# Scores of three attentions in row tiles of 32 or 64 rows, two heads interleaved into two PSUM banks

## The reference, cut to what matters

```python
# layer 0: self attention over 112 tokens, 16 heads of 32, causal; then cross
# attention to a context of 375 positions, 16 heads of 16, no mask
scores = einsum('bhqd,bhkd->bhqk', q * scale, k)        # 112 x 112, then 112 x 375
# layers 1 and 3: cross attention to the same context, 16 heads of 64, key mask
sim = einsum('bhid,bhjd->bhij', q, k)                   # 112 x 375
sim = where(media_mask[:, None, None, :], sim, finfo.min)
attn = softmax(sim, axis=-1)
out = einsum('bhij,bhjd->bhid', attn, v)
```

## Time and profile before

| | |
|---|---|
| median of 3 runs | 2167.96 us (2167.66 to 2169.86) |
| the profiled execution | 2164.93 us, of which its span 2163.1 us |
| PE busy | 1976.2 us, 91% |
| DVE busy | 1286.9 us, 59% |
| POOL busy | 1185.7 us, 55% |
| ACT busy | 917.9 us, 42% |
| mean granted TensorE clock | 0.97 |

### The profile page before, as it was taken

The page is one execution under the profiler, slowest core; times in us unless marked ns, Lnnn a source line. Parts: engine busy times, 40 slices in busy tenths (PEclk is TensorE's granted clock), DMA queues, the critical chain, the costliest instruction groups (busy, mean ns, idle before and its releaser), DMA issues.

```text
span 2163.1 us, 35765 instructions
## 1 busy us (share of the span) xinstructions
PE 1976.2 (91%) x12332; PEld 1725.7 (80%) x12332; DVE 1286.9 (59%) x3174; ACT 917.9 (42%) x2326; POOL 1185.7 (55%) x1357
## 2 busy tenths in 40 slices
PE   4998888988899999999999989998879999998998
PEld 3865576777689998989999978996548999987998
DVE  6777766777545254347888845422175888874422
ACT  2025515555421121137777723222134777771321
POOL 3553417557078899966444336870045545423785
PEclk9999889999899999999999999999999999999999
DMA  3110100001023333321000022332230000001232
GB/s 119 39 55 1 38 15 8 15 21 31 22 76 101 116 109 116 115 76 40 9 20 12 12 82 78 108 108 65 77 102 25 20 13 22 13 2 40 88 108 83
DMA packets 38193, 118.88 MB, mean 55 GB/s; under 512 B 6168, under 2 KB 10264, under 8 KB 38016
## 3 DMA queue, kind: packets, MB, share of 16 engines
q1 hardware_dynamic: 31408, 107.92, 16.0%
q10 hardware_dynamic: 6608, 8.68, 1.3%
HBM read 114.75 MB, written 1.84 MB: 54 GB/s over the span
## 4 chain that ended last, share of the span: by engine, by line
PE 57%; DVE 21%; issue 9%; ACT 7%; POOL 4%; DMA 1%; ACTq 0%; DVEq 0%; SPq 0%; POOLq 0%
PE psum L542 9%; PE psum L543 9%; PE psum L544 9%; PE psum L535 6%; PE psum L804 6%; DVE masked_t L1319 4%; PE psum L658 4%; PE psum L660 4%; PE psum L659 4%; DVE kk L1285 3%; ACT probs_t L988 3%; DVE probs_t L1330 3%; PE psum L761 2%; POOL wl L1631 2%; ACT probsT_t L1006 1%
## 5 line engine op out<-in xcount | busy, mean ns | idle before, releaser
L1631 POOL TENSOR_TENSOR wl<-raw,wh 128x256 fp32r<-128x256 f32 x656 | 517.8, 820 | 13.7
L1623 POOL TENSOR_SCALAR wh<-raw 128x1024 fp32r<-128x1024 f32 x164 | 185.4, 1130 | 329.3 <-PE psum L544 181.5
L542 PE MATMUL psum<-nh,wh 128*128 128x448 f32 x904 | 348.6, 386 | 14.5 <-DVEq L1384 7.8
L543 PE MATMUL psum<-nl,wh 128*128 128x448 f32 x904 | 337.7, 374 | 0.0
L544 PE MATMUL psum<-nh,wl 128*128 128x448 f32 x904 | 337.0, 373 | 0.0
L761 PE MATMUL psum<-cst,probs_t 112*125 112x112 f32 (+1 forms) x1304 | 237.9, 280 | 58.0 <-DVE probs_t L1330 57.6
L988 ACT ACTIVATE probs_t<-masked_t,nmin 112x375 f32<-112x375 f32 (+1 forms) x384 | 205.9, 536 | 181.3 <-DVE nmin L1319 178.4
L761 PEld LDWEIGHTS psum<-cst,probs_t 112*125 112x125 f32 (+1 forms) x1304 | 189.4, 183 | 109.8 <-DVE probs_t L1330 106.1
L1330 DVE TENSOR_SCALAR probs_t<-probs_t,rinv 112x376 f32<-112x376 f32 (+1 forms) x520 | 249.9, 481 | 18.5
L1456 DVE TENSOR_TENSOR hid_l<-scr,hid_h 128x448 fp32r<-128x448 f32 x108 | 93.5, 866 | 229.1 <-ACT hid_h L1063 228.5
L542 PEld LDWEIGHTS psum<-nh,wh 128*128 128x128 f32 x904 | 175.5, 194 | 36.6 <-issue 11.1
(11 more groups left out here) (187 smaller groups left out, 4418.5 us busy)
## 6 DMA issues: line engine op xcount, KB each, us to landing
raw<-in_walls SPq DMA_DIRECT2D x183, 512.0 KB, 3.4
raw<-in_ctxF SPq DMA_DIRECT2D x24, 375.0 KB, 3.0
ctxb<-in_ctxF ACTq DMA_DIRECT2D x8, 375.0 KB, 3.9
ctxt<-in_ctxK ACTq DMA_DIRECT2D x8, 375.0 KB
x<-in_xT ACTq DMA_DIRECT2D x2, 896.0 KB, 11.1
outT<-x SPq DMA_DIRECT2D x2, 896.0 KB, 5.0
mask<-in_kmask ACTq DMA_DIRECT2D x16, 41.0 KB, 2.6
vself<-in_tt SPq DMA_DIRECT2D x1, 448.0 KB, 6.7
```

The source lines that it names most:

```text
L542: nc.tensor.matmul(out, ah, bh, start=(i == 0), stop=False)
L543: nc.tensor.matmul(out, ah, bl, start=False, stop=False)
L1631: last = nc.gpsimd.tensor_tensor(low[cut], src[cut], high[cut].bitcast(F32), ALU.subtract)
```

## The change

- **Row tiles.** The score matmuls of self attention and of the layer 0 cross attention use 32 rows (two heads of 16 share a row tile there, the queries of the other head of the two being zero), those of layers 1 and 3 use 64 rows.
- **Two heads at once.** `scores(a, s)` is called at even steps only (but for the one-head attention of layer 2) and makes steps s and s + 1, their matmuls alternating between the two heads, whose rows lie in different row tiles and whose results lie in the two banks. It waits until both banks are free, that is for step s - 1 instead of s - 2 at the same place. In layers 1 and 3 a head takes three matmuls of 64 rows instead of two of 128.
- **Keys and queries written once.** A K tile in layers 1 and 3 is written by one ACT copy and one DVE subtraction of 128 partitions instead of two of 64 each; a group of queries is split by POOL in two instructions of 128 partitions instead of eight of 64.
- **Layouts.** "mself" is gone (32 POOL instructions, and the wait for it); "mcross" writes two variants (even and odd head) instead of eight, 4 instructions a batch instead of 16.
- In the layer 0 cross attention `head_of` swaps the second and third head of each four, so that the two of a call lie in different row tiles.

```diff
-WORK = (uses("qk") + batches("mself", 0, 1) + uses("v") + batches("ctx0", 0, 1) +
-        batches("mself", *range(2, B)) + uses("dense") + uses("kv0") + uses("cq") + batches("mcross", 0, 1) +
+WORK = (uses("qk") + uses("v") + batches("ctx0", 0, 1) + uses("dense") + uses("kv0") + uses("cq") + batches("mcross", 0, 1) +
...
+        def head_of(a, s):
+
+            h = s % a.nh
+            return h // 4 * 4 + (0, 2, 1, 3)[h % 4] if a is att_c0 else h
...
                 if s >= 2:
 
-                    pe.wait_ge(a.maxed if a.mask else a.exped, s - 1)
-                if a is att_c0:
-                    product3(s_bank(s)[:, 0:376], ops).then_inc(a.scored, 1)
-                elif a.k_heads:
-                    product(s_bank(s)[:, 0:376], ops).then_inc(a.scored, 1)
-                else:
-                    product(out, ops).then_inc(a.scored, 1)
+                    pe.wait_ge(a.maxed if a.mask else a.exped, s)
+                wide = a.nk + a.nk % 2
+                passes = [(0, 0), (0, 1), (1, 0)] if a.k_heads else [(0, 0)]
+                for n, (i, j) in enumerate(passes):
+                    for t in (s, s + 1):
+                        h = head_of(a, t)
+                        if a is att_self:
+                            rows = slice(32 * (h % 4), 32 * (h % 4) + 32)
+                            q, k = qT[rows, h // 4, bcols(b)], kT[rows, h // 4, bcols(b)]
+                        elif a is att_c0:
+                            rows = slice(32 * (h % 8 // 2), 32 * (h % 8 // 2) + 32)
+                            q, k = qmx[rows, b % 2, i, h // 8, h % 2, :], keys_of(a, s // 8)[rows, j, :]
+                        else:
+                            rows = slice(64 * (h % 2), 64 * (h % 2) + 64)
+                            q, k = (qd, ql)[i][rows, s // 8 % 2, h // 2 % 4, :], keys_of(a, s // 2)[rows, j, :]
+                        last = nc.tensor.matmul(s_bank(t)[:, 0:wide], q, k, start=(n == 0), stop=(n == len(passes) - 1))
+                        if n == len(passes) - 1:
+                            last.then_inc(a.scored, 1)
...
-                        scores(a, s)
+                        if a is att_2 or s % 2 == 0:
+                            scores(a, s)
...
-                    if a is att_c0:
-                        nc.scalar.copy(kk[:, i % 2, 0, :], bank[:, 0:376]).then_inc(a.k_high, 1)
-                    else:
-                        for h in range(2):
-                            own = slice(64 * h, 64 * h + 64)
-                            last = nc.scalar.copy(keys_of(i)[own, h, :], bank[own, 0:376])
-                        last.then_inc(a.k_high, 1)
+                    nc.scalar.copy(keys_of(a, i)[:, 0, :], bank[:, 0:376]).then_inc(a.k_high, 1)
...
+                own = keys_of(a, i)
+                last = nc.vector.tensor_sub(own[:, 1, :], bank[:, 0:376], own[:, 0, :].bitcast(F32))
                 last.then_inc(emptied["dve"], 1)
...
+                src, high = q1[:, 4 * g:4 * g + 4, bcols(b)], qd[:, i % 2]
+                nc.gpsimd.tensor_scalar(high, src, 1.0, 1.0, ALU.mult, ALU.mult).then_inc(split_h, 1)
+                pool.wait_ge(split_h, n_split + 1)
+                nc.gpsimd.tensor_tensor(ql[:, i % 2], src, high.bitcast(F32), ALU.subtract).then_inc(split_l, 1)
...
-                    work = [(qmx[:, b % 2, i, :, j, :], t[:, :, bcols(b)].bitcast(F32), C_H8 + j)
-                            for j in range(8) for i, t in enumerate((qch, qcl))]
+                work = [(qmx[:, b % 2, i, :, j, :], t[:, :, bcols(b)].bitcast(F32), (C_EVEN, C_ODD)[j])
+                        for j in range(2) for i, t in enumerate((qch, qcl))]
```

More of the change, by code:

```diff
@@ L338, in build @@
         ttT_in = sem("ttT_in")
-        q_step = sem("q_step")
         laid_out = sem("laid_out")
@@ L716, in scores @@
                 b, h = s // a.nh, s % a.nh
-                out = s_bank(s)[:, 0:a.nk]
-                if a is att_self:
-                    ops = [(qm[:, b % 2, h // 4, h % 4, :], kT[:, h // 4, bcols(b)])]
-                elif a is att_c0:
-                    q = [qmx[:, b % 2, i, h // 8, h % 8, :] for i in range(2)]
-                    k = [kk[:, s // 8 % 2, i, :] for i in range(2)]
-                    ops = [(*q, *k)]
-                elif a is att_2:
-                    ops = [(hw[:, k, bcols(b)], ctxb[:, b % 2, k, 0:S2]) for k in range(KC)]
-                else:
-                    high_q, low_q = [t[:, s // 8 % 2, h % 2, h // 2 % 4, :] for t in (qd, ql)]
-                    k = keys_of(s // 2)[:, h % 2, :]
-                    ops = [(high_q, k), (low_q, k)]
                 if h == 0:
@@ L743, in scores @@
                     tile_done(pe, (a.name, "K", s // a.k_heads, 0))
[L744 to L752 removed]
+                if a is att_2:
+                    if s >= 2:
+                        pe.wait_ge(a.exped, s - 1)
+                    product(s_bank(s)[:, 0:a.nk], [(hw[:, k, bcols(b)], ctxb[:, b % 2, k, 0:S2]) for k in range(KC)])\
+                        .then_inc(a.scored, 1)
+                    return
+                if s >= 2:
+                    pe.wait_ge(a.maxed if a.mask else a.exped, s)
[16 more added lines that the diff above has]
+                            last.then_inc(a.scored, 1)
             def turn(a, s):
@@ L793, in weigh @@
                     return
-                for pair in ((0, 2), (1, 3)) if a is att_c0 else ((0, 1), (2, 3)):
+                for pair in ((0, 1), (2, 3)):
                     for c in range(CH):
                         for i in pair:
-                            h = h0 + i
+                            h = head_of(a, s0 + i)
                             pT = probsT[(s0 + i) % NTURN][0:KEYS, c * S:(c + 1) * S]
@@ L1279, in project @@
                 dve.wait_ge(a.k_high, i + 1)
-                if a is att_c0:
-                    last = nc.vector.tensor_sub(kk[:, i % 2, 1, :], bank[:, 0:376], kk[:, i % 2, 0, :].bitcast(F32))
-                else:
-                    for h in range(2):
-                        own, other = slice(64 * h, 64 * h + 64), slice(64 - 64 * h, 128 - 64 * h)
-                        last = nc.vector.tensor_sub(keys_of(i)[other, h, :], bank[own, 0:376],
-                                                    keys_of(i)[own, h, :].bitcast(F32))
+                own = keys_of(a, i)
+                last = nc.vector.tensor_sub(own[:, 1, :], bank[:, 0:376], own[:, 0, :].bitcast(F32))
                 last.then_inc(emptied["dve"], 1)
@@ L1568, in split_queries @@
                     pool.wait_ge(ATT[name[-1]].scored, 8 * (i - 1))
-                def step(ins):
-                    steps[0] += 1
-                    ins.then_inc(q_step, 1)
-                    pool.wait_ge(q_step, steps[0])
                 if n_split >= 1:
                     pool.wait_ge(split_l, n_split)
-                for h in range(2):
-                    own, other = slice(64 * h, 64 * h + 64), slice(64 - 64 * h, 128 - 64 * h)
-                    src = q1[own, 4 * g:4 * g + 4, bcols(b)]
-                    step(nc.gpsimd.tensor_scalar(qd[own, i % 2, h], src, 1.0, 1.0, ALU.mult, ALU.mult))
-                    step(nc.gpsimd.tensor_scalar(qd[other, i % 2, h], src, 1.0, 1.0, ALU.mult, ALU.mult))
@@ L1582, in split_queries @@
-                nc.gpsimd.sem_inc(split_h, 1)
-                for h in range(2):
-                    own, other = slice(64 * h, 64 * h + 64), slice(64 - 64 * h, 128 - 64 * h)
-                    src, high = q1[own, 4 * g:4 * g + 4, bcols(b)], qd[own, i % 2, h].bitcast(F32)
-                    step(nc.gpsimd.tensor_tensor(ql[own, i % 2, h], src, high, ALU.subtract))
-                    step(nc.gpsimd.tensor_tensor(ql[other, i % 2, h], src, high, ALU.subtract))
-                nc.gpsimd.sem_inc(split_l, 1)
+                src, high = q1[:, 4 * g:4 * g + 4, bcols(b)], qd[:, i % 2]
```

32 lines of the change are left out of this document (10 added, 22 removed).

## The result

The changed kernel takes **2154.06 us** (median of 7 runs, 2152.32 to 2160.55) against 2167.66 us (2159.38 to 2169.86) for the kernel before in the same measurement: ratio 0.9953, 95% interval 0.9933 to 0.9973. It is faster, by half a per cent where I forecast 1.4%. The profiled execution took 2153.12 us, its span 2151.3, against 2163.1 before.

A forecast was written before the change was run, and what follows sets the result against it. PE bounds layers 1 and 3, a PE-DVE-ACT loop layer 0's cross attention, DVE nearly self attention. -12 - 0.5 + 0 - 9 - 8 = -29.5 off the 2167.96 median gives 2138 us; own range 2115 to 2155, 8 in 10 2095 to 2185.

The forecast's parts named there:

- So 3.5 against 3.53: I take 0, and 8 us either way: Layer 0's cross attention: the loop through PE, DVE and ACT takes 3.5 us a pair against 3.53 before, no gain.
- My condition for being wrong: Layer 0's cross attention: the forecast is wrong if its loop runs above 3.7 us a pair.
- rival 4: Score banks no longer decouple, DVE and PE take turns; layer 0's cross attention +11 to +24, about 2168 us; chance 0.05.
- Self attention, -12 and -0.5 for the start: Half of DVE's 25.0 us wait for scores goes (-12); fewer POOL layout instructions bring layer 0's first scores 0.5 us earlier.
- Layers 1 and 3, -9 and -8: Net change of the two cross attentions: 15 us more PE work each, less 24 and 23 us of waits.
- +15 a layer: Layers 1 and 3: row tiles cost PE 1.78 us a pair against 1.54, times 64 pairs.
- The waits were to give back 24 and 23: Layers 1 and 3: PE's weight loads stop waiting for ACT's copies and DVE's scalings, 23.9 and 22.6 us.
- DVE loses one of the two subtractions: Layers 1 and 3: one 547 ns subtraction less per K tile, 35 us of DVE's 239, as a reason the waits go.
- Do two tiles run at once?: Scores on row tiles: two tiles were taken to overlap almost fully, the second head's passes 0.03 us behind the first's.
- Rival 1: Row tiles take turns: +20 and +21 us in layers 1 and 3, +20 in layer 0, 2223 us; chance 0.18.
- Rival 2: Weight loads of the six score matmuls take turns: +9, +9 and +5 in the cross attentions, 2161 us; chance 0.15.
- rival 3: Changing to row tiles costs nothing: 0.28 us less a pair, -18 in each of layers 1 and 3, 2102 us; chance 0.12.

The follow-up runs named there:

- The filler: Changed kernel plus two unread 376-column matmuls ahead of each transpose group in layer 0's cross attention: 2153.21 us, ratio 0.9950.

## Why the prediction was right and wrong

The direction and the range were right, the size was not: 2154 measured, 2138 forecast. That it still lies inside my own range, 2115 to 2155, is luck: layer 0's cross attention lies 14 us beyond its bound of 8, and some 8 us outside the attentions, which I had not forecast, went the other way.

- **The step that failed: "So 3.5 against 3.53: I take 0, and 8 us either way", layer 0's cross attention.** Measured +21.8 us, 3.91 a pair. The walk round the loop was sound and even a little pessimistic: 3.38 at full clock. What it left out is that every duration in it came from rows at a clock of 1.00, and that the change itself moved the clock; the term for that was nothing, without a reason. PE ran at 1.2 GHz for 88 us of the stage, in eight falls, 34 us in all. Scores on 32 rows are what let it, since 64 rows with the same work and waits take 13 to 23 us less. I had read PE's 199.5 of 226.1 us as room to spare. My condition for being wrong, a loop above 3.7 us a pair, is met, but rival 4, which has it, names another cause, K, V and output work that does not hide; at full clock that work hides well enough.
- **Self attention, -12 and -0.5 for the start.** 10.8 measured, with the clock of its window at 0.87 instead of 0.94. In the ten further profiles with the same self attention the first cross scores start at 329.0 to 335.8 us, against 347.0 and 347.4 in the two with the old one: 11 to 18 us. Right, if anything too small.
- **Layers 1 and 3, -9 and -8.** 8.7 and 6.2 measured. The windows are 279 and 278 where I said 277 and 281, but the window of layer 3 in the earlier trace rows starts 6 us ahead of its first scores; from first scores to last `weigh` it was 284.2, and my 8 less would be 276. The sums came out within 2 us; their terms less so. PE's cost of row tiles was put at +15 a layer and is 9 us by windows (10.4 to 11 by PE's busy time, 272.0 against 261.0 and 261.6). The waits were to give back 24 and 23, and pairing gave 17.8 and 15.0. I had put the whole of the loads' waits, 23.9 us, on the window, but PE itself was idle for only 13.4 of layer 1's 280.6 us (busy 267.18); the rest of the 17.8 came off its busy time. Two errors of some 6 us stood against each other, which is luck too. Of my two reasons, "DVE loses one of the two subtractions" explains nothing, as the run with both shows; the other, the two results ready together, does it.
- **Do two tiles run at once?** Yes, as forecast: 0.50 us a pair is lost when they may not. Rival 1 is out. Rival 2 too: four loads take 0.27 us together, and the last two matmuls start 0.96 behind the transposes' load (forecast 0.97, with loads in turn 1.13). And rival 3: 0.52 in and 0.26 idle behind.
- **Outside the attentions** some 8 us fewer, which I had not forecast, in four stretches of 1.1 to 2.7 us. Two of them, 2.1 and 2.7 us, are more than the 2 us that I had named as a sign of being wrong. The stretch between layer 0's cross attention and layer 1's first scores takes 404.8 us before, 402.6 after, and 398.7 in a run that leaves it as before. I put the 8 down to the play between executions; it was not tested.

The Trainium skill ("TensorE: Matmul & The Clock Gate", Part 1) says that the clock is set by how busy PE has been. A reading of busy time alone does not fit here: with one 32-row head a call the clock fell behind stretches at full clock in which PE was busy 91 to 97%, and with pairs over 128 rows it held for 199 us at 84%. The same page, Part 3, says that matmuls start in strict program order; the trace of the kernel with one head behind the other shows two row tiles starting side by side against the program's order, and the measurement decides, while "TensorEngine Tiling (Array Packing)", Key Properties, calls tiles independent, and the two runs on overlap agree with that.

What stays open: why layer 0's stage still shows 0.90 to 0.97 with 64 rows, whether it is the number of rows or the tile mode that counts, and how much it counts beside the idle time. The filler raised the clock with 32-row scores in place, and doubled rows raised it with the idle time in place; I have no run that parts the two further.

## What to carry to other kernels

A change that takes work off TensorE where it has time to spare can slow it down, as it did here. Where TensorE is not full, look at the granted clock of that window in the new profile before trusting durations from the old one, and try the wider tile (here 64 rows with zeros took 226 to 238 us, 32 rows 250 to 255, in the same stage). Split a change into its scheduling part and its layout part before keeping both: here issuing two heads in one call gave 33 us, and the row tiles that came with it took 18 back in the same two layers. A row tile pays only when the passes it saves take longer than two changes of tiling, some 0.3 us here.

## What the runs showed of the hardware that I had not expected

- With the same matmuls, columns and waits, doubling the rows of the score tiles with zeros moved the granted clock of a stage from 0.82 to 0.96.
- With one 32-row head a call the clock fell behind full-clock stretches with PE busy 91 to 97% (0.76 in the stage); pairs over 128 rows held it for 199 us at 84%. Layers 1 and 3, with 64-row scores and PE busy throughout, had 1.00.
- Two row tiles overlap whether the program alternates them or not: 272.0 us interleaved, 272.4 one head behind the other, 304.3 in one tile.
- At half clock six row-tiled matmuls take 1.28 us instead of 0.77, and `weigh` 2.46 instead of 1.34.
